# Second layer's expert slots: gate and up weights copied per slot and held stationary, rows moving

## The reference, cut to what matters

```python
for e in range(num_experts):                       # 8 experts
    h = jax.nn.silu(x @ w_gate[e]) * (x @ w_up[e]) # x: 2048 x 128, h: 2048 x 512
    out = out + w_full[:, e:e + 1] * (h @ w_down[e])
hs = jax.nn.silu(x @ ws_gate) * (x @ ws_up)        # the shared expert
out = out + hs @ ws_down
```

## Time and profile before

| | us |
|---|---|
| median of 3 runs (716.35 to 718.37) | 716.82 |
| the profiled execution | 718.9 |
| its span, first to last instruction | 717.0 |
| layer 1: first gather issued | 549.7 |
| layer 1: first slot's rows turned | 553.2 |
| layer 1: last slot's result copied to `yout` | 686.1 |

### The profile page before, as it was taken

How to read it: one execution, slowest core, us unless ns; L and a number is a source line. 1 busy time by engine, 2 the same in 40 slices (tenths; PEclk the granted TensorE clock), 3 DMA queues, 4 the chain that set the end, 5 groups by cost and what they waited for, 6 DMA issues and landing times.

```text
span 717.0 us, 8658 instructions
## 1 busy us (share of the span) xinstructions
PE 578.1 (81%) x2522; PEld 343.5 (48%) x2522; DVE 413.8 (58%) x725; ACT 354.6 (49%) x626; POOL 384.9 (54%) x306
## 2 busy tenths in 40 slices
PE   6978779877888839769868976978784999999981
PEld 3657446655566414224323422433453576666650
DVE  2454771010003889999989998999477232222236
ACT  3444244443443375964875596668040344334433
POOL 1011226656662316895797689678432465655352
PEclk9999899999999969989988999999988999999996
DMA  3244001111113944434344335443000111111142
GB/s 103 86 138 148 16 15 43 44 35 46 39 37 94 377 173 146 146 139 153 123 137 145 117 123 188 124 134 141 0 16 15 34 38 42 35 36 38 27 120 61
DMA packets 35147, 65.77 MB, mean 92 GB/s; under 512 B 6111, under 2 KB 23207, under 8 KB 34464
## 3 DMA queue, kind: packets, MB, share of 16 engines
q1 hardware_dynamic: 29824, 51.19, 21.3%
q0 software_dynamic: 4992, 9.32, 5.1%
q10 hardware_dynamic: 288, 4.72, 1.8%
HBM read 57.60 MB, written 8.52 MB: 92 GB/s over the span
## 4 chain that ended last, share of the span: by engine, by line
PE 46%; issue 16%; DVE 15%; ACT 10%; POOL 6%; DMA 4%; another core or an unknown queue 1%; SPq 0%; POOLq 0%; DVEq 0%; ACTq 0%
PE ps L619 10%; PE ps L636 9%; PE ps L628 5%; PE ps L621 4%; PE ps L739 4%; PE ps L684 4%; DVE wide L1440 4%; POOL wide L1596 3%; DVE w L1440 2%; ACT work L1039 2%; POOL w L1596 2%; DVE ps L1433 2%; DVE work L1350 1%; DMA w<-bc_rows 1%
## 5 line engine op out<-in xcount | busy, mean ns | idle before, releaser
L1623 POOL DMA_INDIRECT rows<-xn_rows,source x78 | 76.1, 975 | 61.4 <-DVE dest L1287 38.2
L1440 DVE TENSOR_TENSOR_SCAN wide<-work,ps 128x1024 f32<-128x1024 f32 x43 | 98.2, 2284 | 1.3
L1308 DVE COPY xT<-ps 128x128 f32<-128x128 f32 x78 | 22.6, 292 | 114.3 <-PE ps L613 52.2
L739 PE MATMUL ps<-wide,ident 128*128 128x512 f32 x128 | 68.8, 665 | 22.0 <-POOL wide L1596 22.0
L1433 DVE TENSOR_TENSOR ps<-ps,w 128x1024 f32<-128x1024 f32 x64 | 78.9, 1233 | 10.2 <-DMA w<-bc_rows 3.8
L739 PE MATMUL ps<-w,ident 128*128 128x512 f32 x128 | 64.8, 630 | 19.6 <-POOL w L1596 19.6
L1313 DVE TENSOR_TENSOR wide<-wide,ps 128x512 f32<-128x512 f32 x39 | 26.9, 689 | 77.9 <-ACT wide L921 65.8
L1039 ACT ACTIVATE work<-work,a_neg 128x512 f32<-128x512 f32 x86 | 56.8, 711 | 26.0 <-DVE wide L1440 23.5
L1596 POOL TENSOR_TENSOR wide<-wide,w 128x1024 f32<-128x1024 f32 x22 | 51.9, 2361 | 31.7 <-DVE wide L1440 31.4
L1629 POOL DMA_INDIRECT y_choice<-yout,dest x40 | 40.4, 1010 | 47.1 <-ACT yout L835 32.4
L628 PEld LDWEIGHTS ps<-ident,wide 128*128 128x128 f32 x312 | 38.4, 141 | 44.6 <-issue 41.3
(11 more groups left out here) (249 smaller groups left out, 1135.6 us busy)
## 6 DMA issues: line engine op xcount, KB each, us to landing
w<-bc_rows SPq DMA_DIRECT2D x64, 512.0 KB, 3.7
w<-in_w ACTq DMA_DIRECT2D x2, 2304.0 KB, 9.6
w<-y_choice SPq DMA_DIRECT2D x16, 256.0 KB, 3.7
wg<-in_wg SPq DMA_DIRECT2D x1, 2304.0 KB, 11.1
wu<-in_wu SPq DMA_DIRECT2D x1, 2304.0 KB, 16.1
wd<-in_wd SPq DMA_DIRECT2D x1, 2304.0 KB, 21.0
rows<-xn_rows,source POOLq DMA_INDIRECT x78
work<-in_x SPq DMA_DIRECT2D x4, 256.0 KB, 2.7
```

What stands on the lines that cost most here:

```text
L739: last = mm_(bank(6 + h), ident[:, :], hc[j % 4][:, h, :], start=False, stop=(j == NS - 1))
L1440: V.tensor_tensor_scan(st[n % 3].rearrange("p h t -> p (h t)"), dA[n % 3].rearrange("p h t -> p (h t)"), dbu.rearrange("p h t -> p (h t)") ...
L1623: G.indirect_dma_start(out=xin[i % RING][:, :], out_offset=None, in_=xn_rows, in_offset=bass.IndirectOffsetOnAxis(ap=source[:, i:i + 1], a ...
```

## The change

In layer 1 the roles of the operands are exchanged. The 128-column pieces of gate and up weights are the stationary operand and `xT` moves, so that the product comes out with the hidden values on the partitions, as the down projection needs it. Line 628 and its copy to `hT` go away in layer 1. The stationary operands are read at a fixed place: for each slot ACT copies the expert's 512 columns of `wg` to `own_g` (in the space of `hT`), DVE those of `wu` to `own_u` (in the space of `ga`), each reading `slot_e` into a register first. The pipeline is a step shorter: PE's step i takes the down projection of slot i. The two PSUM banks that held the turned inner rows now serve as a second bank each for the turned input and for the result. Layer 0 computes as before.

```diff
-        x_bank, y_bank = ((0, 6), (0, 0)), ((1, 7), (1, 1))
+        x_bank, y_bank = ((0, 6), (0, 3)), ((1, 7), (1, 2))
# PE
+                def step_fixed(i):
+                    x, h, y = i + 2, i + 1, i
+                    if valid(x):
+                        q = x % RING
+                        pe.wait_ge(*xin_loaded[1][q].at((x // RING + 1) * 16))
+                        wait_pos(pe, xT_set[1], x - 1)
+                        tr(bank(x_bank[1][x % 2], P), xin[q][:, 0:D], ident[:, :]).then_inc(x_ps[1].sem, 1)
+                    if valid(h):
+                        p = h % 2
+                        pe.wait_ge(*xT_set[1].at(h + 1))
+                        pe.wait_ge(own_g_set, h + 1)
+                        wait_pos(pe, th_set[1], h - 1)
+                        for j in range(HB):
+                            last = mm_(ps[:, hbank[0] + p, j * P:(j + 1) * P], own_g[p][:, j * P:(j + 1) * P], xT[p][:, :],
+                                       start=True, stop=True)
+                        last.then_inc(g_ps, 1)
+                        pe.wait_ge(own_u_set, h + 1)
+                        wait_pos(pe, hs_set[1], h - 1)
+                        for j in range(HB):
+                            last = mm_(ps[:, hbank[1] + p, j * P:(j + 1) * P], own_u[p][:, j * P:(j + 1) * P], xT[p][:, :],
+                                       start=True, stop=True)
+                        last.then_inc(h_ps[1].sem, 1)
+                    if valid(y):
+                        p = y % 2
+                        e = expert_of(y)
+                        pe.wait_ge(*hs_set[1].at(y + 1))
+                        wait_pos(pe, yout_set[1], y - 1)
+                        for j in range(HB):
+                            last = mm_(bank(y_bank[1][p], D), hs[p][:, j * P:(j + 1) * P], wc[:, ds(e + j * D, D)],
+                                       start=(j == 0), stop=(j == HB - 1))
+                        last.then_inc(y_ps[1].sem, 1)
# ACT
+                def own_weights(i):
+                    wait_pos(act, h_ps[1], i - 1)
+                    e = act.value_load(slot_e[0:1, i:i + 1], min_val=0, max_val=NE * HID)
+                    cp(own_g[i % 2], wg[:, ds(e, HID)]).then_inc(own_g_set, 1)
+
+                def step_fixed(i):
+                    h, y = i + 1, i
+                    if valid(h):
+                        p = h % 2
+                        act.wait_ge(g_ps, h + 1)
+                        wait_pos(act, hs_set[1], h - 1)
+                        A(th[p], bank(4 + p), ACT.Silu).then_inc(th_set[1].sem, 1)
+                    if valid(y):
+                        q = y % RING
+                        act.wait_ge(*y_ps[1].at(y + 1))
+                        wait_pos(act, ys_sent[1][q], y // RING * 16)
+                        cp(yout[q][:, :], bank(y_bank[1][y % 2], D)).then_inc(yout_set[1].sem, 1)
+                    if valid(i + 3) and i >= -1:
+                        own_weights(i + 3)
# DVE
+                def own_weights(i):
+                    wait_pos(dve, h_ps[1], i - 1)
+                    e = dve.value_load(slot_e[0:1, i:i + 1], min_val=0, max_val=NE * HID)
+                    V.tensor_copy(own_u[i % 2], wu[:, ds(e, HID)]).then_inc(own_u_set, 1)
                     if l and valid(h):
                         p = h % 2
                         dve.wait_ge(*th_set[l].at(h + 1))
-                        wait_pos(dve, hT_ps[l], h - 1)
+                        dve.wait_ge(*h_ps[l].at(h + 1))
+                        wait_pos(dve, y_ps[l], h - 1)
                         V.tensor_tensor(hs[p], th[p], bank(6 + p), ALU.mult).then_inc(hs_set[l].sem, 1)
+                    if l and valid(i + 3) and i >= -1:
+                        own_weights(i + 3)
```

More of the change, by code:

```diff
@@ L169, in build @@
         th, ga, hs, hT = ([wide[:, (2 * j + k) * HID:(2 * j + k + 1) * HID] for k in range(2)] for j in range(4))
+        own_g, own_u = hT, ga
         yout = [sb(f"yout{k}", [P, D]) for k in range(4)] + [pre[:, k, :] for k in range(4)]
@@ L282, in build @@
         x_ps = layers("x_ps", ROUTED); xT_set = layers("xT_set", ROUTED)
-        h_ps = layers("h_ps", ROUTED); th_set = layers("th_set", 0)
+        own_g_set = sem("own_g_set"); own_u_set = sem("own_u_set"); g_ps = sem("g_ps"); h_ps = layers("h_ps", ROUTED); th_set = layers("th_set", 0)
         hs_set = layers("hs_set", ROUTED); hT_ps = layers("hT_ps", ROUTED)
@@ L611, in step @@
                         pe.wait_ge(*xin_loaded[l][q].at((x // RING + 1) * 16))
-                        wait_pos(pe, xT_set[l], x - 1 + l)
+                        wait_pos(pe, xT_set[l], x - 1)
                         tr(bank(x_bank[l][x % 2], P), xin[q][:, 0:D], ident[:, :]).then_inc(x_ps[l].sem, 1)
@@ L619, in step @@
                         last = mm_(bank(hbank[0] + p), xT[p][:, :], wa[:, ds(e, HID)], start=True, stop=True)
-                        if wb is not None:
-                            last = mm_(bank(hbank[1] + p), xT[p][:, :], wb[:, ds(e, HID)], start=True, stop=True)
                         last.then_inc(h_ps[l].sem, 1)
@@ L633, in step @@
                         pe.wait_ge(*hT_set[l].at(y + 1))
-                        wait_pos(pe, yout_set[l], y - 1 + l)
+                        wait_pos(pe, yout_set[l], y - 1)
                         for j in range(HB):
@@ L638, in step @@
                         last.then_inc(y_ps[l].sem, 1)
-                slot_steps(step)
+                slot_steps(step_fixed if l else step)
             moe(0)
@@ L918, in step @@
                         act.wait_ge(*h_ps[l].at(h + 1))
[L919 to L924, removed]
+                        wait_pos(act, hT_ps[l], h - 1)
+                        A(hs[p], bank(4 + p), ACT.Silu).then_inc(hs_set[l].sem, 1)
                     if valid(t):
@@ L941, in moe @@
                 if l:
+                    act.wait_ge(*expert_set[1].at(1))
+                    own_weights(0)
+                    own_weights(1)
                     act.wait_ge(*sT_set[1].at(3 * HB))
@@ L1321, in moe @@
                 gating()
+                if l:
+                    dve.wait_ge(*expert_set[1].at(1))
+                    dve.wait_ge(*sT_set[1].at(3 * HB))
+                    own_weights(0)
+                    own_weights(1)
                 slot_steps(step)
```

## The result

| | before | changed |
|---|---|---|
| median, us (20 runs each) | 717.32 (716.35 to 719.53) | 714.49 (711.57 to 719.87) |
| profiled execution, us | 718.9 | 711.57 |
| first gather to first result copied | 15.98 | 13.37 |
| first to last result copied (38 intervals) | 120.44 | 119.44 |
| slots 10 to 30, from turn to turn | 3.29 | 3.34 |

A forecast was written before the change was run, and what follows sets the result against it. PE's own work was taken as the bound, with held signals taking part back: 6.7 us less over the 38 intervals and 2.5 at the start, 9.2 in all, give 709.7 profiled, 707.6 median; range 699 to 716.

The forecast's parts named there:

- PE's slot: Layer 1's expert slots: turn, gate and up, down projection take PE 2.80 us instead of 3.16, 0.36 less.
- weight loads hidden: Gate and up on PE: 16 passes at 0.112 us, 1.79 in all, with their loads beside them.
- copies and reads hidden in a calm slot: ACT and DVE: weight copies and 0.6 us reads cost nothing; ACT stands at 2.1 us, DVE at 2.0, under 2.80.
- the first result 2.5 us earlier: Start of layer 1's slots: first result copied 2.5 us earlier, between 0 and 4.
- signals held because of POOL's indirect DMAs: Layer 1's middle slots: back-to-back indirect DMAs hold PE's signals from about the eighth slot to the 31st; chance 0.50.
- 22 slots at layer 0's steady 3.13, 16 at 2.80, sum 113.7: Layer 1's 38 intervals: 68.9 us with held signals plus 44.8 without, against 120.4 before, 6.7 less.
- The price taken from layer 0: Layer 1's middle slots were given layer 0's steady 3.13 us each, four slots in 12.50 us.
- Not on the path: PE's waits for the two weight copies: PE comes 2.8 us later, a read and a copy take 1.2.
- PE throughout: Rival: PE sets the pace in all of layer 1's slots, 106.4 us instead of 120.4; 700.3 us, chance 0.20.
- Copies as the pace: Rival: a 2 us read on ACT makes its slot about 3.15 us; 714 us, 712 to 717, chance 0.17.
- The slower rival: DVE's copy and POOL's indirect DMAs block each other, 0.37 us per DMA, slots of 3.55; 723 us, chance 0.09.
- two rules of the Trainium skill: Loads overlap only between different row groups, 1.7 us more per slot; DVE's float32 SBUF copies and GpSimd's descriptor writes exclude each other.

The follow-up runs named there:

- a_deep2: a_deep run again, four buffers for each copied weight against the changed kernel's two, chip of 718.04 us: 717.61 us, 0.9989 of the kernel before.
- a_deep: Changed kernel with four buffers instead of two for each copied weight, copied a slot earlier; chip of 694.40 us: 679.63 us, 0.9776 of the kernel before.
- a_pause_s: Changed kernel with POOL clearing two columns behind each layer 1 scatter, waited for; chip of 694.40 us: 680.74 us, 0.9804 of the kernel before.
- a_nocopy: Changed kernel without the weight copies and their register reads on ACT and DVE, PE taking expert 0's gate and up weights: 712.77 us, 0.9916 of before.
- a_deep_pause: Changed kernel with four buffers per copied weight and a two-column pause behind each scatter, chip of 718.04 us: 713.25 us, 0.9944 of the kernel before.
- a_paced: Changed kernel with POOL clearing 32 columns behind each indirect DMA of layer 1, waited for: 714.03 us, 0.9931 of the kernel before.
- a_p295: Changed kernel with POOL clearing 384 columns behind each layer 1 scatter, waited for; chip of 720.64 us: 715.13 us, 0.9911 of the kernel before.

## Why the prediction was right in part and wrong in size

Right: PE's slot (2.80 forecast, 2.79 measured); weight loads hidden; copies and reads hidden in a calm slot (0.43 and 0.63 us, reads 0.3 to 0.35, where 0.6 was taken); the first result 2.5 us earlier (15.98 to 13.37 us behind the first gather, 2.6); signals held because of POOL's indirect DMAs.

Wrong: the term "22 slots at layer 0's steady 3.13, 16 at 2.80, sum 113.7". The 38 intervals between first and last result took 119.4: 1.0 less than before, where 6.7 less were forecast. That is the whole miss, since the start gave what it should. By the turns of line 614: slots 8 to 30 (646.75 - 573.17) took 73.6 us, 3.34 each, and not 68.9: 4.7 more. The 13 intervals around them (3 to 8 and 30 to 38) took 39.5 us, and not 36.4: 3.1 more, since holds were there at both ends and not only in the middle. The run-out behind the last turn took 2.1 less than its share. 4.7 + 3.1 - 2.1 = 5.7, and 119.4 - 113.7 = 5.7.

The price taken from layer 0 was the wrong neighbour. In the cycle of the changed kernel above POOL idles behind four DMAs and not behind eight as in the earlier trace rows, so two slots take 6.77 us where four took 12.50. Layer 1's own late slots stood beside it at 3.35, and the prediction read them as a loss on 3.16 which a shorter slot could shrink. They were already close to the limit: with 3.35 for the 22 slots the prediction's own sum is 118.5. Two indirect DMAs a slot gave a middle of 3.31 to 3.55 us in the changed kernel and all its variants with at most 0.3 us of spacing in a pair on chips that hold signals, and 3.29 in the kernel before, which needs 0.37 more on PE. That is one indirect DMA in 1.65 to 1.75 us (POOL's 21st to 61st start of the layer). Fewer DMAs took PE's own time: 2.79 and 3.16. So before, 16 calm slots at 3.16 ran ahead of that pace and the later ones fell behind it; changed, the holds start in the first slots. That the calm slots run up a debt which the later ones pay is a reading that no run tests. Of 35 x 0.37 = 13 us that PE needs less between turn 3 and turn 38, 1.6 came out (114.7 to 113.1). The other 2.0 of the 3.6 us lie at the ends: from turn 38 to the last result 6.9 us instead of 9.8, from the first gather to turn 3 12.8 instead of 12.0.

"Not on the path", said of the waits for the copies, was wrong behind a held signal: 0.96 us of PE at 600.91. But it cost little, since taking it away (a_deep2) moved the idle elsewhere.

PE throughout (700.3) was no error of mechanism: it is what happens on the chips without held signals, 2.0 to 2.2% in a_deep and a_pause_s. The changed kernel itself wasn't run there. Copies as the pace (714) stands at the measured time by luck: ACT's slot is about 1.8 us (0.58 + 0.28 + 0.35 + 0.63).

The slower rival fell by its price and not by its mechanism. It put off each DMA by 0.37 us. In the changed kernel 4 of the 78 DMAs take 1.08 to 1.17 us (all others but the first stay under 1.05), and 3 of DVE's 39 copies take 0.50 to 0.73 instead of 0.43; all seven overlap a copy or a DMA of the other engine. Without the copies (a_nocopy, and the kernel before) no DMA but the layer's first is over 1.05. In a_deep it is 14 scatters in a row, by 0.2 us each. Most copies that start while a DMA runs leave both as they were, and the held signals have nothing to do with it: they are there in a_nocopy as well (middle 3.35).

Of the two rules of the Trainium skill that spoke against the change one holds. "TensorE: Matmul & The Clock Gate", The mechanism, lists that a load overlaps only between different row groups: the trace disagrees, 16 passes and their loads take 1.79 us, 0.112 each, on all 128 rows. The same section also has loads pulled ahead of running matmuls when they go to the background weight buffer, which the prediction left out and which the trace doesn't contradict. "SBUF — State Buffer", Who interferes with whom, has a float32 copy on DVE and GpSimd's descriptor writes wait for each other: the trace agrees in kind, with the 1.20 us scatters of a_deep and the copies of 0.50 to 0.73 us above, but the waits are few in the changed kernel and at most about 0.3 us each, and no slot became longer by them in a_deep.

Open: why some chips hold signals, and whether it is the chip at all or its state at the time, since each chip was seen in one round of runs; what the pace is made of, since spacing a pair to 2.90 us leaves it and to about 3.4 ends the holds; why the same two DMAs a slot settle at 3.13 us in layer 0 and at 3.3 and more in layer 1; and whether scatters alone bring it. No version that computes the whole was clearly faster than the changed kernel on a chip that holds signals: a_deep_pause, a_paced and a_p295 overlap with it.

## What to carry to other kernels

Before pricing a shorter slot, find the slots that already run slower than the bounding engine's own work, and take their time as the floor of the new slot until something shows otherwise; a price from a neighbouring stage is second best. Count indirect DMAs per slot as a resource of their own: here, where signals are held, one and a half a slot were free and two were the bound, and POOL's busy time (49 of 82 us) did not show it; on the other chips two were free and three were the bound. And run the control on the same chip: nearly the same edit was worth 0.5% on one chip and 2.2% on another.

## What the runs showed of the hardware

- PE's semaphore signals can come 0.5 to 4.9 us late when indirect DMAs of POOL follow each other at 1.3 us; two that come due 0.1 us apart come out within 0.04 us of each other (599.56 and 599.60). It differed between chips: with before at 717 to 721 us they were held in every kernel with two DMAs a slot but the one spaced to about 3.4 us a pair (a_paced), with before at 694 in none of the five profiled ones with two or three, at equal times of the gathers themselves (975 ns in most on both).
- A copy of 128x512 float32 from SBUF to SBUF on DVE and an indirect DMA of POOL put each other off at times: a scatter that starts 0.10 to 0.12 us behind the copy takes 1.20 to 1.22 us instead of 1.02 (14 in a_deep), and a copy takes up to 0.73 us instead of 0.43 (at 590.27 in the changed kernel, 0.53 us into a scatter). A copy that starts 0.08 to 0.10 us into a gather changes neither (0.43 and 0.97 us).
- The same layer 0 took 3.13 us a slot on the one kind of chip and 2.34 on the other, which is 20 of the 23 us between them (its last turn at 194.9 in a_deep against 215.1 in the kernel before, its first at 104.5 and 104.0).
- Clearing 32 columns behind a gather cost POOL 0.65 us in all (0.14 and a gap of 0.81 in place of 0.30), behind a scatter 0.1 in most, 0.3 in some.
